# One graph-network kernel on one core: a third of an edge count moved into pauses of two later stages, edge terms computed beside the graph tables, and hops that begin with three blocks

## The reference, cut to what matters

```python
# first block, for two layers (4 heads, then 1 head)
te = relu(edge_attr @ We + be) * exp(x @ Wo + bo)[src][:, None]      # per edge
al = leaky_relu((hx.a_s)[src] + (hx.a_d)[dst] + ((te @ Wge).a_e))    # "edge terms" feed this
al = softmax of al over the edges of one dst
out = segment_sum(hx[src] * al, dst)                                 # gather rows, weigh, add
# second block: a mixture of 8 experts on every node
# third block: 5 hops on the graph, self loops added
for _ in range(5):
    h = segment_sum(norm * h[col], row)      # here a matrix of edge counts times h
    acc += sigmoid(h @ lin_w + lin_b) * h
# fourth block: attention over slices
```

## Time and profile before

| what | value |
|---|---|
| median of 3 runs | 4129.83 us (4128.82 to 4133.42) |
| the profiled execution, its own time | 4126.51 us |
| span of its records | 4124.9 us |
| granted TensorE clock, mean over the span | 0.861 |
| PE busy | 2775.6 us (67%) |
| PEld busy | 1806.5 us (44%) |
| DVE busy | 2122.7 us (51%) |
| ACT busy | 616.6 us (15%) |
| POOL busy | 1025.5 us (25%) |

### The profile page before, as it was taken

The page is one execution under the profiler, slowest core; times in us unless marked ns, Lnnn a source line. Parts: engine busy times, 40 slices in busy tenths (PEclk is TensorE's granted clock), DMA queues, the critical chain, the costliest instruction groups (busy, mean ns, idle before and its releaser), DMA issues. The chain is left out here.

```text
span 4124.9 us, 63590 instructions
## 1 busy us (share of the span) xinstructions
PE 2775.6 (67%) x16126; PEld 1806.5 (44%) x16126; DVE 2122.7 (51%) x4893; ACT 616.6 (15%) x1333; POOL 1025.5 (25%) x987
## 2 busy tenths in 40 slices
PE   2568886561177656028863597069999999997677
PEld 1134443450155435015543376036565656564345
DVE  7557776694388548226633000844444444443553
ACT  0345554100011000000001121310000000000221
POOL 0000000376287745767770200100000000000000
PEclk9989999875599877569985799589999999998887
DMA  1211112452144336235546232231212121212001
GB/s 66 72 36 40 44 44 74 158 171 75 47 114 120 111 109 214 80 108 157 157 139 240 98 108 100 81 118 54 99 56 97 57 97 59 97 57 81 0 2 42
DMA packets 206558, 379.27 MB, mean 92 GB/s; under 512 B 35807, under 2 KB 155344, under 8 KB 203222
## 3 DMA queue, kind: packets, MB, share of 16 engines
q1 hardware_dynamic: 120090, 188.27, 13.1%
q0 software_dynamic: 50384, 139.33, 11.8%
q10 hardware_dynamic: 35968, 50.35, 3.5%
HBM read 270.37 MB, written 108.29 MB: 92 GB/s over the span
## 5 line engine op out<-in xcount | busy, mean ns | idle before, releaser
L1907 PE MATMUL hop_wide<-hop_hs,counts 128*128 128x512 bf16 x3125 | 1025.9, 382 | 197.5 <-DMA hop_hs<-hop_parts 190.0
L654 POOL DMA_INDIRECT gat_ring<-hx_rows,src_i x784 | 836.0, 1066 | 312.9 <-issue 247.3
L1908 PE MATMUL hop_narrow<-hop_hs,counts 128*128 128x256 bf16 x3125 | 855.9, 274 | 0.0
L1907 PEld LDWEIGHTS hop_wide<-hop_hs,counts 128*128 (+1 forms) x3125 | 307.1, 98 | 577.7 <-issue 215.2
L925 PE MATMUL cnt_acc<-cnt_oh_src,cnt_oh_dst 128*128 x1960 | 375.0, 334 | 117.9 <-DVE cnt_oh_src L855 63.5
L855 DVE TENSOR_SCALAR cnt_oh_src<-cnt_number,cnt_column 128x1600 f16 (+1 forms) x490 | 309.7, 633 | 136.3 <-PE cnt_acc L925 102.8
L1305 PE MATMUL agg_acc<-agg_msg,agg_oh 128*128 x976 | 265.1, 423 | 102.2 <-DVE agg_oh L1239 102.1
L1880 DVE TENSOR_SCALAR hop_h<-hop_narrow,all_dis 128x256 f32<-128x256 f32 x125 | 60.5, 484 | 529.9 <-PE hop_narrow L1908 529.9
L1908 PEld LDWEIGHTS hop_narrow<-hop_hs,counts 128*128 (+1 forms) x3125 | 307.2, 98 | 36.3
L925 PEld LDWEIGHTS cnt_acc<-cnt_oh_src,cnt_oh_dst 128*128 x1960 | 189.7, 97 | 287.7 <-issue 200.8
L1305 PE MATMUL agg_acc<-gat_ring,agg_oh 128*128 x976 | 262.1, 411 | 71.0 <-DVE agg_oh L1236 66.5
(11 more groups left out here) (407 smaller groups left out, 3627.9 us busy)
## 6 DMA issues: line engine op xcount, KB each, us to landing
look_part<-src_low SPq DMA_DIRECT2D x28, 896.0 KB
hop_hs<-hop_parts POOLq DMA_DIRECT2D x25, 960.0 KB, 6.1
hop_parts<-hop_parts SPq DMA_DIRECT2D x125, 192.0 KB, 1.9
count_rows<-cnt_out SPq DMA_DIRECT2D x50, 400.0 KB, 2.4
counts<-count_rows ACTq DMA_DIRECT2D x5, 4000.0 KB, 30.7
exp_w<-in_L_ffn_w SPq DMA_DIRECT2D x16, 1024.0 KB, 9.9
hop_acc<-x_gcn SPq DMA_DIRECT2D x125, 128.0 KB, 2.0
x_gcn<-hop_acc SPq DMA_DIRECT2D x125, 128.0 KB, 1.8
```

Source lines behind the costliest of these rows:

```text
L654: pool.indirect_dma_start(out=self.ring[:, t % RING, :], out_offset=None, in_=self.g.hx_rows, in_offset=bass.IndirectOffsetOnAxis(ap=self. ...
L1907: pe.matmul(wide[i][:, :], count, hs[:, t, 0:2 * D], start=(t == 0), stop=(t == NB - 1))
L1908: mm = pe.matmul(narrow[i][:, 0:D], count, hs[:, t, 2 * D:3 * D], start=(t == 0), stop=(t == NB - 1))
```

## The change

1. `constants` no longer fills DRAM with zeros. SP does so in `graph_tables`, beside the histograms, from a tile that POOL clears.
2. `edge_terms` runs in `graph_tables`. ACT does all four Relus and the copy, DVE none of it; PE does one edge round after every one or two groups of the histogram, and the store of the terms ends with that stage.
3. The count is a class, `Counter`. Stage `counts` does windows 0 to 33 (`MAIN` = 34). Windows 34 to 49 are done four at a time (`EACH` = 4) in the two pauses of `edge_weights` of each layer, on one set of PSUM banks, with ACT storing them by its own queue. In each visit the half with two operations of DVE comes first, ACT makes its Abs before it waits for the buffer, and with two bank sets it does two visits before it copies out the window before.
4. `RING` is 112 tiles, and `AHEAD` is lower: 56 pairs at every point of layer 0, and 34, 42, 46, 56 in layer 1.
5. Each hop begins with blocks 0, 1 and 2 together, chunk by chunk, on three pairs of banks; the 22 others follow two by two on two pairs, and the last block now has the other pair than block 0.

```diff
-RING = 140
+RING = 112
...
-            @block.sync
-            def _(sp):
-                sp.wait_ge(filled, after(1))
-
-                sp.dma_start(g.edge_fill.rearrange("(p j) c -> p (j c)", p=P)[:, 0:2048], zero[:, :]).then_inc(filled, 16)
-                sp.dma_start(g.edge_fill.rearrange("(p j) c -> p (j c)", p=P)[:, 2048:ET * SW],
-                             zero[:, 0:ET * SW - 2048]).then_inc(filled, 16)
-                per = NE * SLOTS * D // P // 2048
-                for k in range(per):
-                    sp.dma_start(g.expert_in.rearrange("(p j) c -> p (j c)", p=P)[:, k * 2048:(k + 1) * 2048],
-                                 zero[:, :]).then_inc(filled, 16)
-                sp.wait_ge(filled, after(1 + 16 * (2 + per)))
 
 
...
+                edges["load"](sp)
+                all_filled = fill_with_zeros(sp)
...
+                edges["store"](sp)
                 sp.wait_ge(src_kept, after(32))
+                sp.wait_ge(filled, all_filled)
...
+                edges["vector"](dve)
...
-                by_halves(pe, group)
+                edge_round = edges["tensor"](pe)
+                done = 0
+                for n in range(ET // GRP):
+                    group(n, n % 2)
+                    if (n + 1) * edges["rounds"] // (ET // GRP) > done:
+                        edge_round(done)
+                        done += 1
...
+    def on_scalar(act):
+
         def copy_out(r):
-            dve.wait_ge(downed, after(r + 1))
-            dve.tensor_copy(terms[:, cols(r)], down[r % 2][:, 0:WIDE]).then_inc(copied, 1)
-
-        for r in range(ROUNDS):
-            dve.wait_ge(upped, after(r + 1))
-            if r >= 2:
-                dve.wait_ge(downed, after(r - 1))
-            dve.tensor_scalar(hid[2][r % 2], up[2][:, 0:WIDE], be[:, 0:1], 0.0, ALU.add, ALU.max).then_inc(dve_hid, 1)
-            dve.tensor_scalar(hid[3][r % 2], up[3][:, 0:WIDE], be[:, 0:1], 0.0, ALU.add, ALU.max).then_inc(dve_hid, 1)
-            if r:
-                copy_out(r - 1)
-        copy_out(ROUNDS - 1)
-
-    def on_scalar(act):
+            act.wait_ge(downed, after(r + 1))
+            act.activation(terms[:, cols(r)], down[r % 2][:, 0:WIDE], ACT.Copy).then_inc(copied, 1)
+
         for r in range(ROUNDS):
             act.wait_ge(upped, after(r + 1))
             if r >= 2:
                 act.wait_ge(downed, after(r - 1))
-            act.activation(hid[0][r % 2], up[0][:, 0:WIDE], ACT.Relu, bias=be[:, 0:1]).then_inc(act_hid, 1)
-            act.activation(hid[1][r % 2], up[1][:, 0:WIDE], ACT.Relu, bias=be[:, 0:1]).then_inc(act_hid, 1)
+            for k in range(GROUPS):
+                act.activation(hid[k][r % 2], up[k][:, 0:WIDE], ACT.Relu, bias=be[:, 0:1]).then_inc(act_hid, 1)
+            if r:
+                copy_out(r - 1)
+        copy_out(ROUNDS - 1)
...
+        def edge_round(r):
+            pe.wait_ge(act_hid, after(GROUPS * (r + 1)))
             if r + 1 < ROUNDS:
                 hidden(r + 1)
             outcome(r)
...
-    AHEAD = ((60, 70, 70, 70), (34, 42, 46, 58))
+    AHEAD = ((56, 56, 56, 56), (34, 42, 46, 56))
...
+    MAIN, EACH = 34, 4
...
+        self.bank_set = [w % 2 if w < self.MAIN else 0 for w in range(NW)]
+        self.turn = [self.bank_set[:w].count(self.bank_set[w]) for w in range(NW)]
...
+    def on_vector(self, dve, windows):
+
+        def visit(p, w, then=None):
+
+            found = None
+            slot = (p + w) % 2
+            for k in (1, 0):
+                dve.wait_ge(self.used[k], after(p + w))
+                if k:
+                    dve.tensor_scalar(self.oh_dst(k, slot), self.half16[:, :], at(self.key, 2 * p + k),
+                                      self.minus_first[:, w:w + 1], ALU.subtract, ALU.is_equal)
+                dve.tensor_scalar(self.oh_src(k, slot), self.number[:, :], at(self.column, 2 * p + k), None,
+                                  ALU.is_equal).then_inc(self.hot[k], 1)
+                if then and k:
+                    found = then()
+            return found
+
+        first = self.bound(dve, windows[0])
+        for w in windows:
+            last = visit(first, w, lambda: self.bound(dve, w + 1))
+            with dve.If(last > first):
+                with dve.Fori(first + 1, last + 1) as p:
+                    visit(p, w)
+            first = last
...
+    def on_scalar(self, act, windows, whole, stores):
+
+        def visit(p, w):
+            slot = (p + w) % 2
+            act.wait_ge(self.hot_a, after(p + w))
+            act.activation(at(self.apart, slot), self.nodes[:, w % 2, :], ACT.Abs, bias=at(self.key, 2 * p)
+                           ).then_inc(self.far, 1)
+            act.wait_ge(self.far, after(p + w + 1))
+            act.wait_ge(self.used[0], after(p + w))
+            act.activation(self.oh_dst(0, slot), at(self.apart, slot), ACT.Relu, scale=-2.0,
+                           bias=self.g.ones[:, 0:1]).then_inc(self.hot_a, 1)
+
+        def evict(w):
+            i, o = self.bank_set[w], w % 2
+            act.wait_ge(self.summed[i], after(self.turn[w] + 1))
+            act.wait_ge(self.stored[o], after(16 * (w // 2)))
+            act.activation(self.out[o][:, :].rearrange("p (n c) -> p n c", n=self.BANKS), whole[i][:, :, 0:self.COLS],
+                           ACT.Copy).then_inc(self.read[i], 1)
+            if stores:
+                self.store(act, w)
+
+        first = self.bound(act, windows[0])
+        for w in windows:
+            act.activation(self.nodes[:, w % 2, :], self.minus_half[:, :], ACT.Identity, bias=self.minus_first[:, w:w + 1]
+                           ).then_inc(self.numbered_a, 1)
+            last = self.bound(act, w + 1)
+            act.wait_ge(self.numbered_a, after(w + 1))
+            visit(first, w)
+            two_sets = w > windows[0] and self.bank_set[w - 1] != self.bank_set[w]
+            if two_sets:
+                with act.If(last > first):
+                    visit(first + 1, w)
+            if w > windows[0]:
+                evict(w - 1)
+            with act.If(last > first + 1 if two_sets else last > first):
+                with act.Fori(first + (2 if two_sets else 1), last + 1) as p:
+                    visit(p, w)
+            first = last
+        evict(windows[-1])
...
+    def on_tensor(self, pe, windows, whole):
+
+        def edge_products(i, start):
+            for n in range(self.BANKS):
+                mm = pe.matmul(whole[i][:, n, 0:1], self.zero16[:, 0:P], self.zero16[:, 0:1], start=start, stop=not start,
+                               skip_group_check=True)
+            return mm
+
+        first = self.bound(pe, windows[0])
+        for w in windows:
+            i = self.bank_set[w]
+            pe.wait_ge(self.read[i], after(self.turn[w]))
+            edge_products(i, True)
+            last = self.bound(pe, w + 1)
+            with pe.Fori(first, last + 1) as p:
+                slot = (p + w) % 2
+                for k in (1, 0):
+                    pe.wait_ge(self.hot[k], after(p + w + 1))
+                    if not k:
+                        pe.wait_ge(self.hot_a, after(p + w + 2))
+                    for n in range(self.BANKS):
+                        mm = pe.matmul(whole[i][:, n, 0:self.COLS], self.oh_dst(k, slot),
+                                       self.oh_src(k, slot)[:, n * self.COLS:(n + 1) * self.COLS],
+                                       start=False, stop=False, skip_group_check=True)
+                    mm.then_inc(self.used[k], 1)
+            edge_products(i, False).then_inc(self.summed[i], 1)
+            first = last
...
+        windows = range(c.MAIN)
...
+        whole = [s.ps("acc", (P, counter.BANKS, 512))]
+        begin = counter.MAIN + 2 * counter.EACH * layer
+        before_nodes = range(begin, begin + counter.EACH)
+        before_fill = range(before_nodes.stop, before_nodes.stop + counter.EACH)
...
                 dve.sem_inc(scanned, 1)
+                counter.on_vector(dve, before_nodes)
 
                 dve.wait_ge(gathered, 16 * NB)
...
                 dve.sem_inc(weighed, 1)
+                counter.on_vector(dve, before_fill)
 
                 dve.wait_ge(spread, after(16))
...
+                counter.on_scalar(act, before_nodes, whole, True)
                 act.wait_ge(weighed, after(1))
                 act.activation(g.w_self[:, :, 0:H], self_v[:, :, :], ACT.Exp).then_inc(exp_done, 1)
+                counter.on_scalar(act, before_fill, whole, True)
...
                     mm.then_inc(returned, 1)
+                    if not n:
+                        counter.on_tensor(pe, before_nodes, whole)
+                        counter.on_tensor(pe, before_fill, whole)
...
+    TOGETHER = 3
+    ROUNDS = (NB - TOGETHER) // 2
...
+        together = [(b, b % 2, b // 2, b, 0) for b in range(TOGETHER)]
...
+        def couple(j):
+            return [(3 + 2 * j, 1, 1 + j, 0, 1 + j), (4 + 2 * j, 0, 2 + j, 1, 1 + j)]
...
+                    for c in range(NB // CHUNK):
```

(26 more changed lines are left out.)

269 lines of the change are left out of this document (119 added, 150 removed).

## The result

The changed kernel takes 3929.86 us, the kernel before 4131.27 beside it: ratio 0.9512, interval 0.95 to 0.9523. Forecast was 3938. The profiled execution has a span of 3927.4 us against 4124.9, 197.5 less where the sum said 190.1. The terms did not all come out: two are off by 11 and 22 us, in opposite directions.

What follows compares the result with a forecast made beforehand. It took PE to bound the count, closely followed by DVE, and gathers the end of `aggregate` 0. Terms summed to -190.1 from 4126.5, giving 3936.4; with the median 3.3 above, about 3938 us, range 3890 to 4015 (its own 3915 to 3965).

Steps and rivals of the forecast that it cites:

- term 1: Before the count: no zero fill, edge rounds of 3.5 us inside `graph_tables`, store 31.9; first visit at 157.9, -71.5 us.
- Term 2: 33 windows in `counts`: PE stays the bound, two visits ahead of the eviction remove a wait, 0.23 each, -7.6 us.
- 3 16 windows fewer: End of `counts`: 16 windows leave the stage, only the last eviction, store and barrier remain, -146.7 us.
- Term 4: Pauses of `edge_weights`: four windows stick out by 3 to 9 us and slow POOL's transfers, +30.3 us in all.
- Terms 5 and 6: `aggregate` 0 and 1: fewer gathers done ahead, and gathers bound the stage's end, +38 and +15.6 us.
- 7 `hops`: Hop boundaries: three blocks per chunk close PE's gaps and keep its clock up, -48.2 us.
- B: Pauses: PE's clock stays at its lower level, a window takes 17.5 us; 4001 us, chance 10%.
- C: Pauses: they hide all the windows, POOL and DVE hardly meet; 35 us less, 3903, chance 13%.
- D: Pauses: POOL stands while windows run, about 32 us more per pause; 4065 us, chance 5%.
- F: `graph_tables`: edge rounds of 4.3 us, 22 us more; 3960 us, chance 8%.
- G: Count visits: DVE and PE take turns, 3.6 us instead of 1.78, slower than before; about 4370 us, chance 3%.
- E: `aggregate` stages: late gathers cost nothing because DVE and PE find slack; 3884 us, chance 5%.

Runs made afterwards that it cites:

- run 7: The kernel before with only the ring (112 tiles instead of 140) and the counts ahead lowered: 4175.87 us, ratio 1.0119.
- run 9: The changed kernel with the `hops` function of the kernel before: 3979.38 us, ratio 0.9637; `hops` 1089.8 against 1038.4 us.
- run 4: The changed kernel with the store of the edge terms in three pieces instead of one: 4486.62 us, ratio 0.9726, on the slower chip; `graph_tables` 24.5 us less.
- Run 2: The changed kernel with one-hots in four tiles of their own instead of one: 4500.12 us, ratio 0.9763, on the slower chip; `counts` 332.1 instead of 342.9.
- run 1: The changed kernel with the halves of a visit in their old order, half 0 first: 4501.03 us against 4612.41, ratio 0.9754, on the slower chip.
- run 5: The changed kernel once more, unedited, on another chip than the slower one: 3929.12 us against 4128.57 for the kernel before, ratio 0.9523.
- runs 1 to 4: Four variants of the changed kernel (half order, four one-hot tiles, three windows per pause, store in pieces), made together on a slower chip; kernel before 4612.41 us there.

## Why the prediction was right, and where its terms were not

| term | forecast | measured |
|---|---|---|
| 1 until the count starts | -71.5 | -69.7 (159.61 for 229.35) |
| 2 windows in `counts` | -7.6 | +3.0 for 33, +0.4 for the first |
| 3 16 windows fewer | -146.7 | -146.9 |
| 4 `edge_weights` 0 and 1 | +19, +11 | +9.2, -1.3 |
| 5 `aggregate` 0 | +38 | +37.9 |
| 6 `aggregate` 1 | +15.6 | +15.1 |
| 7 `hops` | -48.2 | -47.9 |
| 8 the rest | 0 | +2.8 |

**Terms 1, 3, 5, 6 and 7** came out within 2 us. Terms 5 and 6 are shown by run 7, 7 by run 9 and by the busy window at the boundary. In term 1 the rounds were 3.37 instead of 3.5, but the first of them came at 21.8 instead of 19.9 and the count 40.4 us after the last copy instead of 37.6, so errors of 2 to 4 us cancelled. The forecast let that store stand as given; run 4 showed that it was the largest thing left in the stage. Moving the zero fill was free: `constants` went from 20.9 to 6.7 us, and no stage waited for it later.

**Term 2 failed in sign.** The step was "PE stays the bound; two visits ahead of the eviction take away a wait". PE does stay the bound and the wait did go; but PE's time per visit was taken as unchanged, and it grew by 0.07 us. `counts` has 169 visits (and the pauses 76; the forecast has 166 and 79), bounded by PE, which turns that into 11 us. Run 2 restores 9.34 per window, run 1 rules out the order of the halves.

**Term 4 was mis-sized**, at +30.3 for +7.9. The step that was too large is "POOL's 25 transfers at 1.25 become about 1.56: +8" a pause. They took 30.9 (gathers) and 31.7 us (scatters) before, and 32.1 to 32.4 and 33.3 to 33.6 with four windows beside them (run 5), 0.05 to 0.08 each and not 0.3; in the first profile of the changed kernel they lost 1.2 to 2.3 us a pause. The forecast had the pauses at about 48.5, 48.5, 49.4 and 53.1 us. How its 9.4 a pause comes of the 3 to 9 us by which four windows stick out and the 8 of POOL it doesn't show. In the changed kernel they are 44.4, 43.5, 45.3 and 45.5: three end with the windows, at the low end of the forecast's 41.5 to 48.5, the fourth with the transfers, with its windows, of which the last has one visit, done after 35.2. Together they grew by 14.4 and not 35.3, and 6.5 came off outside of them, for which the forecast had 5.

Why POOL lost so little can be seen in the first pause:

```profile
790.18 1.19 DVE L847 TENSOR_SCALAR cnt_oh<-cnt_number,cnt_column 128x1600 f16 x2
790.69 0.94 POOL L1049 DMA_INDIRECT room<-edge_scan,seg_end  x1 [0.30 <-issue]
...
795.59 1.32 DVE L847 TENSOR_SCALAR cnt_oh<-cnt_number,cnt_column 128x1600 f16 x2
795.69 1.34 POOL L1049 DMA_INDIRECT room<-edge_scan,seg_end  x1 [0.30 <-issue]
```

DVE and POOL do meet: 19 to 23 of the 25 transfers of a pause overlap a one-hot. But of the 100 transfers of the four pauses, 69 take no more than 0.05 us longer than before. The 23 that start 0.10 to 0.45 us into a source one-hot (0.64 us) take 0.06 to 0.40 longer, and all but one end 0.81 to 0.85 us after that one-hot does, as the gather of the earlier trace rows ends 0.83 after its operation. Most of those that start earlier or later in it lose nothing. So the forecast took one gather, caught early in an operation of 1.14 us, as the price of every transfer. Why the moment of the start decides is not shown. The rule of the Trainium skill (SBUF — State Buffer, "Who interferes with whom"), by which an operation of DVE in a two-port mode blocks GpSimd as long as it lasts, has the sign right. Read as the forecast read it, POOL adding DVE's whole time, it is far off: 23 to 26 us of one-hots stood beside the 25 transfers of a pause and cost them 1.2 to 2.3.

The errors of terms 2 and 4 have opposite signs, 11.0 and 22.4 us. That the total came within 8 us is in part luck; neither error shows in it.

**The rivals.** B: PE's granted clock was 0.85 over the first pause and 0.92 over the second (windows 774 to 818.5 and 822.5 to 866), and the four windows took 44.4 and 43.5 us and not 70. (Its price is also mis-added: four windows of 17.5 in each pause are 81 us more than the forecast's pauses, 4018 or so, and not 63 and 4001.) C came nearest: the transfers were hardly slowed, though DVE and POOL did meet, and three pauses still grew by 4 to 5 us. D, F and G did not happen (transfers 1.2 to 2.3 us longer and not 32; round 3.37; visits 1.8). E is ruled out by run 7.

## What to carry to other kernels

Work that is put into a pause costs the longer of the two, not the sum: list what fills a pause, find where the last piece just sticks out, and look at each pause by itself, since the last one here had room for a fifth window (moving only that one would save about 9.7 us by the table; it wasn't tried). Memory is a price of such a move: the buffers for it shortened the gather ring, which alone costs 47 us (run 7), about a fifth of what the rest gains (201 + 47). In a loop bounded by PE, look at the time between visits and not just at the matmuls: the layout of an operand's tile was worth 11 us; and when a store or load ends a stage, ask which part of it could have started earlier.

## What the runs showed of the hardware

The kernel before took 4128 to 4131 us in three sessions and 4612 in the one on the chip of runs 1 to 4. The changed kernel took 3929, and four close variants of it 4487 to 4501 there, whereas most stages agreed within about a microsecond (`counts` 343.2 and 342.9, `hops` 1038.3 and 1037.2 in run 1). The difference lies in stages in which POOL sends indirect gathers. The window of `lookup` 0 in run 1, and two rows of PE's timeline in it:

```profile
568.30:869.70 301.40, 115.11 (x1176) 89.60 (x1176) 152.85 (x230) 0.00 (x0) 111.73 (x114) 0.65 0.29 93
```

```profile
643.15 0.27 PE L781 MATMUL look_bank<-look_pieces,look_part 128*128 128x125 bf16 x1 [2.54 <-issue]
645.96 0.26 PE L781 MATMUL look_bank<-look_pieces,look_part 128*128 128x125 bf16 x1 [2.53 <-issue]
```

The stage takes 301.4 us instead of 167.7. PE has the same 1176 matmuls, but for long stretches one starts every 2.8 us, and nothing that the profile shows is waited for ("issue"); POOL meanwhile issues its gathers every 1.25 us as elsewhere. The slow steps last from 603.3 to 726.5 us, and POOL's gathers of this stage start from 571.3 to 713.1: they end within 14 us of each other. The pauses with windows suffered too (231.3 against 176.0 for `edge_weights` 0). That instructions arrive late, as the expectation of run 5 has it, is not shown. The DMA view of 642 to 738 us in run 1 speaks against late fetching, for it has no packet of an instruction queue, though most of the slow steps lie there:

```profile
q0 software_dynamic: 2832, 7.86, 29.7%
q1 hardware_dynamic: 144, 0.92, 2.4%
```

The cause stays open; shown is that it goes with that chip or session and with the stages that gather. There the change was worth about 2.4% (ratio 0.9754 in run 1, whose `counts` is that of the changed kernel) instead of 4.9%; how much of the loss lies in the windows that now run in the pauses and how much elsewhere is open, since the kernel before has no trace there.
